# The second layer's gates, recurrence and merge in another order, queries before values, and split copies, in a four-layer fp32 kernel

## The chip, the cores and the metric

The kernel runs on one core of one Trainium2 chip, as one program. The metric is the device time of one execution in microseconds (us). The kernel before takes 789.82 us, the median of three runs (787.8 to 791.66).

## The reference

A tensor of 2 x 32 x 32 x 64 goes through four layers, each a residual of the last, all in fp32. What the change touches is in three of them:

```python
# second layer: 16 steps of a linear recurrence with constant gates, closed here
forget_gate = sigmoid(x @ Wf + bf + 2.0); input_gate = sigmoid(x @ Wi + bi)
delta = softplus(x @ Wd + bd) * 0.1
inp_r = delta_r * input_gate_r * Bx_r          # Bx = B * x, complex
step: h_r, h_i = fg_r * (Ar*h_r - Ai*h_i) + inp_r, fg_i * (Ar*h_i + Ai*h_r) + inp_i
# third layer: linear attention
q = softmax(q, -1) / sqrt(32); k = softmax(k, 0); out = (k^T v)^T q @ w_out
# fourth layer: four sweeps of attention without a softmax, over the Gram matrix of the tokens
Z = Z + sum_heads (Z Q Z^T)(Z V^T) / (n * heads)
```

## The kernel before, in words

Each engine runs its own list of instructions in the order in which the code of its block gives them, with waits on semaphores written out by hand (`sig(name)`); no scheduler moves anything. What stands late in an engine's list is late, ready or not. A wait is fulfilled when another engine has counted the semaphore up. The on-chip tiles of all stages lie in one array, `area`, and the eight PSUM banks are `ps`; the profile names them by these two words alone.

The first layer (a selective scan, 128 units) takes the first 463 us. The work around the change comes after it:

- **Gates.** VectorE (DVE) normalizes x into `xn1` (L1223). TensorE (PE) makes four products of four matmuls each (L1576 to L1581): `split` (x parted in real and imaginary halves) first, then the delta gate in banks 4 and 5, the forget gate in 0 and 1, the input gate in 2 and 3, and counts `gates_done` after each. ScalarE (ACT) takes Abs, Exp and Ln of the delta gate (L967 to L974), then loads another table of functions and takes the sigmoids of f and i (L975 to L981). The relu part of the softplus is DVE's (L364).
- **Recurrence** (L342 to L413, DVE). Each step is a 2 x 2 real matrix; its trace `tau` and determinant `det` come from the product and sum of the forget gates, and powers and sums of 2, 4, 8 and 16 steps follow by doubling. Squares are ACT's (L991 to L1002). Sums of `m` and `n` go through PE (`add_parts`). `tt` and `stt` issue an operation of two tensors; with `hold` DVE waits until it has ended.
- **Segments.** PE also mixes, between these, four segments of the fourth layer's filter weights (L1592 to L1598), each read out by ACT (`span_out`, L987) before the next one starts.
- **Merge.** `m` and `v` are put back into the layout of x by PE: four matmuls for `m` once all of DVE's closing work but the two products in `v` is done (`joined` 1), then two for each half of `v` (L1607 to L1616). DVE adds the result to x (L1234), PE turns it (L1623), and the third layer's norm begins (L432 to L444) while PE runs six matmuls that nobody reads (`keep_busy`, L1632).
- **Attention.** PE makes the keys' logits (L1638), then queries and values tile by tile in turn (L1645), in two halves. DVE shifts the queries (L1258, L1259), ACT takes Exp (L1025) and copies values (L1023) and turned keys (L1029), DVE makes the shares (L1267 to L1269), and PE turns them (L1668), multiplies by the mixed context (L1676) and turns the result (L1683).
- **Linear layers** (`for l in range(LAYERS)`, L1338, L1051, L1715): a chain of small products with a PSUM read-out behind each: `copy_g` (L479) makes two copies for `g_two` and one for `g_sb`, then PE makes t in bank 3, ACT copies all 512 columns of it (L1053), PE makes s (L1725).

## Time and profile before

| what | value |
|---|---|
| median of three runs | 789.82 us (787.8 to 791.66) |
| the profiled execution: its time, its span | 790.21 us, 788.4 us |
| mean granted clock of TensorE | 0.977 |
| PE busy | 90% of the span |
| VectorE busy | 77% |
| GpSimd, ScalarE busy | 52%, 44% |
| first layer | about 463 us |
| gates, recurrence, merge (463 to 511) | about 48 us |
| attention to its last turned tile (511 to 547) | about 36 us |
| linear layers (598 to 621) | about 23 us |

### The profile page before, as it was taken

The numbers are of one execution on the slowest core, as the hardware profiler recorded it, in microseconds if no ns is written. First come the engines' busy times: TensorE is split into PE (matmuls) and PEld (weight loads), VectorE is DVE, ScalarE is ACT, GpSimd is POOL, SyncE is SP. The second block draws the span as 40 slices with busy tenths as digits, with TensorE's granted clock in tenths as the row PEclk, the third lists the DMA queues.
The fourth block names the chain that finished last, engine by engine and source line by source line (L and its number), as shares of the span: only waits on it lengthen the run. The fifth ranks groups of instructions, "written<-read, shape, count | busy, mean of one in ns | idle before, by whom it ended". The sixth has DMA issues, their size and how long they took to land.

```text
span 788.4 us, 7109 instructions
## 1 busy us (share of the span) xinstructions
PE 713.4 (90%) x2480; PEld 358.9 (46%) x2480; DVE 605.7 (77%) x598; ACT 349.9 (44%) x387; POOL 413.4 (52%) x229
## 2 busy tenths in 40 slices
PE   6979999989899899998988868997798899999997
PEld 4633333333233233333333323465345577777775
DVE  5799999999999999999999948656793543334432
ACT  3676474556754754556544326143103243333331
POOL 3166999998999999899889900000051000000000
PEclk9979999999999999999999989999999999999999
DMA  5134564665554646536465451300730000000000
GB/s 169 62 133 140 185 212 168 220 214 175 187 180 166 236 162 207 197 137 202 157 246 176 159 214 81 106 10 1 281 145 1 1 0 1 1 1 0 0 0 27
DMA packets 30126, 97.76 MB, mean 124 GB/s; under 512 B 4132, under 2 KB 4870, under 8 KB 29358
## 3 DMA queue, kind: packets, MB, share of 16 engines
q1 hardware_dynamic: 30096, 97.38, 35.6%
q8 instruction: 16, 0.26, 0.1%
q14 instruction: 14, 0.11, 0.0%
HBM read 95.78 MB, written 1.59 MB: 123 GB/s over the span
## 4 chain that ended last, share of the span: by engine, by line
PE 42%; DVE 28%; issue 11%; POOL 9%; DMA 5%; ACT 4%; SPq 0%; DVEq 0%; POOLq 0%
PE ps L1765 15%; DVE area L1173 10%; PE ps L1460 6%; POOL area L617 6%; DVE ps L1161 5%; DMA area<-c_rows 4%; PE ps L1483 4%; PE ps L1781 4%; DVE area L1169 2%; DVE area L354 2%; PE ps L1386 2%; PE ps L1404 1%; DVE small L432 1%; POOL area L633 1%; PE ps L1451 1%
## 5 line engine op out<-in xcount | busy, mean ns | idle before, releaser
L617 POOL TENSOR_TENSOR area<-area 128x1024 f32<-128x1024 f32 x127 | 297.7, 2370 | 32.0 <-DVE area L1173 21.4
L1483 PE MATMUL ps<-area,cst 128*128 128x512 f32 x512 | 254.2, 623 | 7.1 <-POOL area L617 6.6
L1173 DVE TENSOR_TENSOR_SCAN area<-area,ps 128x1024 f32<-128x1024 f32 x111 | 249.8, 2275 | 4.1 <-ACT area L809 0.9
L809 ACT ACTIVATE area<-area,floors,par_sb 128x1024 f32<-128x1024 f32 x111 | 133.0, 1235 | 62.2 <-DVE area L1173 55.6
L1483 PEld LDWEIGHTS ps<-area,cst 128*128 128x128 f32 x512 | 89.8, 192 | 119.9 <-issue 95.5
L1161 DVE TENSOR_TENSOR ps<-ps,area 128x1024 f32<-128x1024 f32 x111 | 133.0, 1213 | 4.5 <-PE ps L1451 3.9
L1765 PE MATMUL ps<-stack,sel 128*128 128x512 f32 (+1 forms) x576 | 116.2, 362 | 0.7 <-DVE sel L1366 0.7
L1765 PEld LDWEIGHTS ps<-stack,sel 128*128 128x128 f32 x576 | 97.0, 191 | 19.7 <-issue 1.2
L464 DVE COPY area<-ps 64x1024 f32<-64x1024 f32 x32 | 39.3, 1227 | 73.6 <-PE ps L1781 41.4
L714 POOL COPY area<-area 128x256 f32 (+1 forms) x16 | 6.4, 403 | 131.3 <-PE ps L1781 131.3
L462 ACT ACTIVATE area<-ps 64x1024 f32<-64x1024 f32 x32 | 32.7, 1021 | 95.7 <-PE ps L1765 52.8
L1451 PE MATMUL ps<-stack,sel 32*128 32x512 f32 x222 | 54.1, 498 | 18.0 <-DVE area L1173 17.8
L695 POOL TENSOR_TENSOR area<-area 128x256 f32<-128x256 f32 x8 | 5.8, 728 | 120.5 <-DVE area L1319 120.5
L1451 PEld LDWEIGHTS ps<-stack,sel 32*128 32x128 f32 x222 | 20.3, 186 | 95.8 <-DVE area L1173 53.0
L1460 PE MATMUL ps<-area,cst 128*128 128x512 f32 x112 | 50.2, 600 | 6.3 <-DVE area L1173 6.3
L809 ACT ACTIVATE ps<-area,floors,par_sb 128x1024 f32<-128x1024 f32 x17 | 20.5, 1208 | 79.2 <-DVE area L1173 79.2
L1386 PE MATMUL ps<-cst 128*128 128x512 f32 (+1 forms) x110 | 45.0, 551 | 0.0
L633 POOL TENSOR_TENSOR area<-area 128x1024 f32<-128x1024 f32 x17 | 40.0, 2355 | 0.0
L1169 DVE TENSOR_TENSOR_SCAN area<-ps,area 128x1024 f32<-128x1024 f32 x17 | 38.5, 2267 | 0.0
L1460 PEld LDWEIGHTS ps<-area,cst 128*128 128x128 f32 x112 | 20.6, 190 | 34.8 <-issue 23.2
L1354 DVE TENSOR_TENSOR stack<-area,stack 128x1025 fp32r<-128x1025 f32 x16 | 19.5, 1227 | 14.8 <-ACT stack L1070 14.8
L1386 PEld LDWEIGHTS ps<-cst 128*128 128x128 f32 x110 | 21.9, 207 | 17.7 <-issue 16.5
(310 smaller groups left out, 713.2 us busy)
## 6 DMA issues: line engine op xcount, KB each, us to landing
area<-c_rows SPq DMA_DIRECT2D x145, 512.0 KB, 4.4
area<-phi_scaled SPq DMA_DIRECT2D x1, 4104.0 KB, 24.2
area<-in_m_phi_dram SPq DMA_DIRECT2D x4, 1024.0 KB, 8.2
area<-phi_scaled SPq DMA_DIRECT2D x1, 4096.0 KB, 13.8
area<-in_q_t_dram SPq DMA_DIRECT2D x1, 1024.0 KB, 13.7
c_rows<-tok SPq DMA_DIRECT2D x28, 32.0 KB, 2.8
area<-in_dft_dram SPq DMA_DIRECT2D x1, 784.0 KB
area<-in_m_u_dram SPq DMA_DIRECT2D x1, 768.0 KB, 5.8
```

The lines of the kernel that those rows point to most:

```text
L464: engine.tensor_copy(dst, src).then_inc(sig("filtered_1"), 1)
L617: pool.tensor_tensor(scan_order(prod[:, u % PRODS, :], k), lines(state[:, u % STATES, :], k), lines(c_sb[:, u % COPIES, :], k), MUL).then_ ...
L633: pool.tensor_tensor(aid, aid, u_in[:, n % 2, :], MUL).then_inc(sig("pool_driven"), 1)
L809: act.activation(dst, delta[:, n % 2, :], ACT.Exp, bias=floors[:, k, i:i + 1], scale=par_sb[:, k, i:i + 1]).then_inc(sig("decayed"), 1)
L1161: dve.tensor_tensor(drive_pair(u), drive_pair(u), u_in[:, n % 2, :], MUL).then_inc(sig("driven"), 1)
L1169: dve.tensor_tensor_scan(state[:, u % STATES, :], banks(BANK["a", u]), aid, 0.0, MUL, ADD).then_inc(sig("scanned"), 1)
L1173: dve.tensor_tensor_scan(state[:, u % STATES, :], decay[:, u % DECAYS, :], drive_pair(u), 0.0, MUL, ADD).then_inc(sig("scanned"), 1)
L1386: pe.matmul(ps[:, bank, 0:cols], ident, cst[:, 0:cols], start=True, stop=True)
L1451: mm = pe.matmul(ps[:, BANK["b", u] + h, :], sel[at:at + 32, i, :], b_rows[at:at + 32, n % 2, :], start=True, stop=True)
L1460: mm = pe.matmul(ps[:, BANK["soft", n] + h, :], ident, half(term, h), start=(at == 0), stop=(at == 3))
L1483: mm = pe.matmul(ps[:, 6 + h, :], con("center"), half(prod[:, u % PRODS, :], h), start=(u % (UNITS // 2) == 0), stop=(u % (UNITS // 2) == ...
L1765: mm = pe.matmul(ps[:, 2 + 2 * (g % 2) + y, :].rearrange("p (a n) -> p a n", a=2)[:, :, P * (at - 2 * y):2 * P], xn_hl[:, x_part, j * P:(j ...
```

## The change

Six things, all in the order of work or in who does it:

1. PE runs four matmuls that nobody reads before the product that averages the statistics of x (`pair_mean`) and two after it, and `keep_busy(5, ...)` before the merge has four in place of two.
2. The gates come in the order split, f, i, delta. ACT loads the sigmoids' table at once, takes both sigmoids, loads the other table, then takes Abs, the square of tau, Exp and Ln. DVE's products of f come before the relu, which is written straight into `v`. Since the logarithm now lives longer in `sp_a`, `sum4` and `p4` trade their tile with `r4_sq` and `lam4`, and ACT's square of `r4` waits until the logarithm has been read (`x_parts` 3).
3. `m * sum16` comes two operations earlier and alone counts `joined` 1. PE merges only the first half of `m`; DVE adds its second half to `v` before `joined` 3. Two matmuls fewer, one DVE addition of 512 columns more.
4. The last segment goes behind the merge, in place of five of the six idle matmuls, and its read-out behind ACT's part of the norm.
5. In attention, a half's queries are all made before its values, and the shares of the first half come before the shift of the second. ACT takes Exp of the first half's queries before it copies the values.
6. In the linear layers `g_ready` is counted before the copy into `g_sb`, and t is made in two banks, of which DVE copies one and ACT the other.

```diff
-        sum4, p4 = halves(sp_a)
+        sum4, p4 = halves(xn1)
...
-        r4_sq, lam4 = halves(xn1)
+        r4_sq, lam4 = halves(sp_a)
...
             dve.wait_ge(sig("gates_out"), 1)
-            for half_r in range(2):
-                link(dve.tensor_scalar(sp_r[...], ps[:, 4 + half_r, :], ..., 0.0, ADD, MAX), half_r == 1)
-            dve.sem_inc(sig("x_parts"), 1)
-            dve.wait_ge(sig("gates_out"), 2)
-            tt(v, r, lg, ADD)
-            dve.wait_ge(sig("gates_out"), 3)
             tt(p8_sq, f[:, 0, :], f[:, 1, :], ADD, False)
...
-            dve.wait_ge(sig("gates_out"), 4)
-            tt(v, v, i, MUL, False)
             tt(gap, tau, det, SUB, False)
+            dve.wait_ge(sig("gates_out"), 3)
+            for half_r in range(2):
+                link(dve.tensor_scalar(sp_v[...], ps[:, 4 + half_r, :], ..., 0.0, ADD, MAX), half_r == 1)
+            dve.sem_inc(sig("x_parts"), 1)
...
-            stt(sum8, step4, 1.0, sum4, ADD, MUL, False)
+            dve.wait_ge(sig("gates_out"), 4)
+            tt(v, v, lg, ADD, False)
+            stt(sum8, step4, 1.0, sum4, ADD, MUL)
+            dve.sem_inc(sig("x_parts"), 1)
+            tt(v, v, i, MUL)
...
-            tt(low16, det, sum16, MUL, False)
+            tt(low16, det, sum16, MUL)
+            dve.tensor_tensor(m, m, both(sum16), MUL).then_inc(sig("joined"), 1)
             tt(r16, r16, r8_sq, SUB)
-            tt(m, m, both(sum16), MUL, False)
             tt(low16, r16, low16, SUB)
-            dve.sem_inc(sig("joined"), 1)
-            for half_r in range(2):
-                dve.scalar_tensor_tensor(v[:, half_r, :], low16, 1.0, v[:, half_r, :], ADD, MUL).then_inc(sig("joined"), 1)
+            dve.scalar_tensor_tensor(v[:, 0, :], low16, 1.0, v[:, 0, :], ADD, MUL).then_inc(sig("joined"), 1)
+            stt(v[:, 1, :], low16, 1.0, v[:, 1, :], ADD, MUL)
+            dve.wait_ge(sig("joined"), 1)
+            dve.tensor_tensor(v[:, 1, :], v[:, 1, :], m[:, 1, :], ADD).then_inc(sig("joined"), 1)
...
-                copy(g_two[at, b, at], src[own, own], *extra)
-            copy(g_sb[own, own], src[own, own], *extra).then_inc(sig(f"g_ready_{b}"), 1)
+                ins = copy(g_two[at, b, at], src[own, own], *extra)
+            ins.then_inc(sig(f"g_ready_{b}"), 1)
+            copy(g_sb[own, own], src[own, own], *extra)
...
-                act.activation(t_sb, ps[:, 3, :], ACT.Copy).then_inc(sig("t_out"), 1)
+                act.activation(t_sb[:, 256:512], ps[:, 1, 0:256], ACT.Copy).then_inc(sig("t_out"), 1)
...
+                dve.wait_ge(sig("t_done"), l + 1)
+                dve.tensor_copy(t_sb[:, 0:256], ps[:, 3, 0:256]).then_inc(sig("t_out"), 1)
...
+            keep_busy(BANK["b", UNITS - 1], 4)
             pair_mean(2)
+            keep_busy(BANK["b", UNITS - 1], 2)
             pe.wait_ge(sig("gn_out"), 2)
...
+            def merged(src, r, last):
                 for h in range(2):
...
+                    mm = pe.matmul(ps[:, h, :], merge[:, h, r, :], src[:, r * HALF:(r + 1) * HALF],
+                                   start=not (r or last), stop=(r == 1))
...
+            pe.wait_ge(sig("joined"), 1)
+            merged(sp_m, 0, False)
+            pe.wait_ge(sig("joined"), 2)
+            merged(sp_v, 0, True)
+            pe.wait_ge(sig("joined"), 3)
+            merged(sp_v, 1, True)
...
-            keep_busy(4, 6)
+            segment(3)
+            keep_busy(4, 1)
```

**ACT, from the rstd of x to the first read-out of a segment.** `ps,small` is the forget gate, `ps,vecs` with a wait on `gates_done` the delta or the input gate. Before:

```order
L970 ACTIVATE area<-ps,vecs 128x512 [waits gates_done]
L970 ACTIVATE area<-ps,vecs 128x512
L973 ACTIVATE area<-area 128x1024 [waits gates_out]
L974 ACTIVATE area<-area 128x1024 [waits act_step]
L975 ACT_TABLE_LOAD
L980 ACTIVATE area<-ps,small 128x512 [waits gates_done]
L980 ACTIVATE area<-ps,small 128x512
L980 ACTIVATE area<-ps,vecs 128x512 [waits gates_done]
L980 ACTIVATE area<-ps,vecs 128x512
L982 ACT_TABLE_LOAD
L991 ACTIVATE area<-area 128x1024 [waits trace_set]
```

And now:

```order
L969 ACT_TABLE_LOAD
L974 ACTIVATE area<-ps,small 128x512 [waits gates_done]
L974 ACTIVATE area<-ps,small 128x512
L974 ACTIVATE area<-ps,vecs 128x512 [waits gates_done]
L974 ACTIVATE area<-ps,vecs 128x512
L976 ACT_TABLE_LOAD
L980 ACTIVATE area<-ps,vecs 128x512 [waits gates_done]
L980 ACTIVATE area<-ps,vecs 128x512
L983 ACTIVATE area<-area 128x1024 [waits trace_set]
L985 ACTIVATE area<-area 128x1024 [waits gates_out]
L986 ACTIVATE area<-area 128x1024 [waits act_step]
```

The two table loads stand before and behind the sigmoids as they did, but Abs, Exp and Ln have moved behind them, and the square of tau between Abs and Exp.

**DVE, from the product of bank 2 with f to the join with x.** Before:

```order
L354 TENSOR_TENSOR area<-ps,area 128x1024 [waits x_summed,dve_step]
L354 TENSOR_TENSOR area<-area 128x512 x2
L354 TENSOR_TENSOR area<-area 128x1024 [waits dve_step]
L354 TENSOR_TENSOR area<-area 128x512
L413 SCALAR_TENSOR_TENSOR area<-area 128x512 [waits dve_step]
L413 SCALAR_TENSOR_TENSOR area<-area 128x512
L1234 TENSOR_TENSOR area<-x_res,ps 128x2x128x2 [waits x_summed] x2
```

And now:

```order
L354 TENSOR_TENSOR area<-ps,area 128x1024 [waits x_summed,dve_step]
L354 TENSOR_TENSOR area<-area 128x512
L408 TENSOR_TENSOR area<-area 128x1024 [waits dve_step]
L354 TENSOR_TENSOR area<-area 128x512
L354 TENSOR_TENSOR area<-area 128x512 [waits dve_step]
L411 SCALAR_TENSOR_TENSOR area<-area 128x512 [waits dve_step]
L357 SCALAR_TENSOR_TENSOR area<-area 128x512
L414 TENSOR_TENSOR area<-area 128x512 [waits joined,dve_step]
L1242 TENSOR_TENSOR area<-x_res,ps 128x2x128x2 [waits x_summed] x2
```

The product of 1024 columns that PE waits for first is now the third operation and not the fourth, and an addition of 512 columns has come in before the join.

**DVE, the queries.** L1258 and L1266 are the maxima, L1267 (before) and L1272 (now) the sums of the shares. Before:

```order
L1258 TENSOR_REDUCE small<-ps 128x32 [waits qv_done]
L1259 TENSOR_TENSOR area<-ps,small 128x1024 [waits dve_step]
L1258 TENSOR_REDUCE small<-ps 128x32 [waits qv_done]
L1259 TENSOR_TENSOR area<-ps,small 128x1024 [waits dve_step]
L1262 TENSOR_SCALAR small<-small 128x1 [waits scalar_steps]
L1263 RECIPROCAL small<-small 128x1 [waits dve_step]
L1267 TENSOR_REDUCE small<-area 128x32 [waits q_exp,dve_step]
L1268 RECIPROCAL small<-small 128x32 [waits dve_step]
L1269 TENSOR_TENSOR area<-area,small 128x1024 [waits dve_step]
L1267 TENSOR_REDUCE small<-area 128x32 [waits q_exp]
```

And now:

```order
L1266 TENSOR_REDUCE small<-ps 128x32 [waits qv_done]
L1267 TENSOR_TENSOR area<-ps,small 128x1024 [waits dve_step]
L1272 TENSOR_REDUCE small<-area 128x32 [waits q_exp]
L1273 RECIPROCAL small<-small 128x32 [waits dve_step]
L1274 TENSOR_TENSOR area<-area,small 128x1024 [waits dve_step]
L1266 TENSOR_REDUCE small<-ps 128x32 [waits qv_done]
L1267 TENSOR_TENSOR area<-ps,small 128x1024 [waits dve_step]
L1280 TENSOR_SCALAR small<-small 128x1 [waits scalar_steps]
L1281 RECIPROCAL small<-small 128x1 [waits dve_step]
L1272 TENSOR_REDUCE small<-area 128x32 [waits q_exp,dve_step]
```

The first half's sum, reciprocal and product now stand ahead of the second half's maximum.

## Rows read from the trace of the kernel before

**Rows 1.** The page: busy time of the engines.

```profile
PE 713.4 (90%) x2480; PEld 358.9 (46%) x2480; DVE 605.7 (77%) x598; ACT 349.9 (44%) x387; POOL 413.4 (52%) x229
```

**Rows 2.** Windows: length; PE, PEld, DVE, ACT, POOL busy; granted clock; DMA share; GB/s.

```profile
465.90:472.10 6.20, 4.25 (x10) 1.24 (x12) 1.75 (x5) 0.50 (x2) 0.00 (x0) 0.51 1.00 424
541.00:544.40 3.40, 3.02 (x14) 2.08 (x14) 0.28 (x1) 1.02 (x1) 0.00 (x0) 0.52 0.00 0
485.00:490.00 5.00, 3.60 (x8) 1.33 (x8) 4.78 (x8) 2.61 (x5) 0.00 (x0) 1.00 0.00 0
```

**Rows 3.** Timeline of PE around the gates: start, us, engine, line, count, [idle before].

```profile
460.54 1.02 PE L1571 MATMUL ps<-area,w_out_w 128*64 128x512 f32 x2
...
465.35 0.38 PE L1381 MATMUL ps<-small,cst 128*128 128x2 f32 x2 [3.78 <-DVE small L1098]
467.85 3.68 PE L1579 MATMUL ps<-area,cst 128*64 128x512 f32 x8 [2.11 <-DVE area L1223]
```

**Rows 4.** Timeline of DVE from the copy of x to the join.

```profile
471.57 1.23 DVE L1225 COPY area<-ps 128x1024 f32<-128x1024 f32 x1 [3.78 <-PE ps L1579]
...
477.51 1.22 DVE L354 TENSOR_TENSOR area<-area 128x1024 f32<-128x1024 f32 x1 [0.66 <-ACT area L974]
480.16 2.62 DVE L354 TENSOR_TENSOR area<-area 128x512 f32<-128x512 f32 x4 [1.43 <-ACT area L980]
...
489.39 1.22 DVE L354 TENSOR_TENSOR area<-area,ps 128x1024 f32<-128x1024 f32 x1
...
499.30 1.23 DVE L354 TENSOR_TENSOR area<-ps,area 128x1024 f32<-128x1024 f32 x1
...
503.74 1.29 DVE L413 SCALAR_TENSOR_TENSOR area<-area 128x512 f32<-128x512 f32 x2
510.04 0.69 DVE L1234 TENSOR_TENSOR area<-x_res,ps 128x512 f32<-128x512 f32 x1 [5.01 <-PE ps L1614]
```

**Rows 5.** Timeline of ACT in the same stage.

```profile
477.49 1.28 ACT L975 ACT_TABLE_LOAD   x1
478.79 1.27 ACT L980 ACTIVATE area<-ps,small 128x512 f32<-128x512 f32 x2
```

**Rows 6.** Timeline of PE, recurrence and merge, and of DVE in the norm.

```profile
490.54 3.70 PE L1596 MATMUL ps<-area 128*128 128x512 f32 x8 [1.94 <-ACT area L987]
...
503.83 3.60 PE L1610 MATMUL ps<-area,cst 128*128 128x512 f32 x8
...
512.23 5.32 PE L1386 MATMUL ps<-cst 128*128 128x512 f32 x12
...
516.33 1.29 DVE L444 TENSOR_TENSOR area<-area,small 128x512 f32<-128x512 f32 x2
```

**Rows 7.** Timeline of ACT and PE, queries and values.

```profile
526.13 1.02 ACT L1023 ACTIVATE area<-ps 128x1024 f32<-128x1024 f32 x1
...
533.45 3.81 PE L1662 MATMUL ps<-area 128*128 128x128 f32 x32 [1.21 <-ACT area L1023]
```

**Rows 8.** Timeline of DVE, keys maximum, shares of the queries, next normalization.

```profile
523.99 0.15 DVE L1245 TENSOR_SCALAR small<-small 128x1 f32<-128x1 f32 x1
...
533.54 1.22 DVE L1259 TENSOR_TENSOR area<-ps,small 128x1024 f32<-128x1024 f32 x1
...
539.48 1.22 DVE L1269 TENSOR_TENSOR area<-area,small 128x1024 f32<-128x1024 f32 x1
...
547.23 0.89 DVE L432 BATCH_NORM_STATS2 small<-ps 128x6 f32<-128x64 f32 x6 [4.17 <-PE ps L1683]
```

**Rows 9.** Timeline of ACT and DVE in the third linear layer.

```profile
609.83 0.45 DVE L488 COPY area<-ps 64x64 f32<-64x64 f32 x2 [0.58 <-PE ps L1736]
...
611.73 0.60 ACT L1053 ACTIVATE area<-ps 128x512 f32<-128x512 f32 x1 [1.33 <-PE ps L1718]
...
614.61 0.29 DVE L1348 COPY area<-ps 128x128 f32<-128x128 f32 x1 [0.58 <-PE ps L1731]
```

**Rows 10.** DMA issues in 463.4:464.0, m_phi's last: KB, us to landing.

```profile
area<-in_m_phi_dram SPq DMA_DIRECT2D x1, 1024.0 KB, 11.2
```

More of the change, by code:

```diff
@@ L965, in pairs @@
                 return t.rearrange("p (r n) -> p r n", r=2)
-            act.wait_ge(sig("gates_done"), 2)
-            for r in range(2):
-                bias = vecs[:, V_BD + r:V_BD + r + 1]
-                ins = act.activation(pairs(sp_a)[:, r, :], ps[:, 4 + r, :], ACT.Abs, bias=bias)
-            ins.then_inc(sig("gates_out"), 1)
-            act.wait_ge(sig("gates_out"), 1)
-            link(act.activation(sp_a, sp_a, ACT.Exp, scale=-1.0))
-            act.activation(sp_a, sp_a, ACT.Ln, bias=1.0).then_inc(sig("gates_out"), 1)
             act.preload_act_table_set("sigmoid_and_others")
             for g, (dst, col) in enumerate(((sp_f, None), (sp_i, V_BI))):
-                act.wait_ge(sig("gates_done"), 3 + g)
+                act.wait_ge(sig("gates_done"), 2 + g)
                 for r in range(2):
@@ L982, in _ @@
             act.preload_act_table_set("natural_log_exp_and_others")
+            act.wait_ge(sig("gates_done"), 4)
+            for r in range(2):
+                bias = vecs[:, V_BD + r:V_BD + r + 1]
+                ins = act.activation(pairs(sp_a)[:, r, :], ps[:, 4 + r, :], ACT.Abs, bias=bias)
+            ins.then_inc(sig("gates_out"), 1)
+            act.wait_ge(sig("trace_set"), 1)
+            act.activation(sp_o, sp_d, ACT.Square).then_inc(sig("trace_sq"), 1)
+            act.wait_ge(sig("gates_out"), 3)
+            link(act.activation(sp_a, sp_a, ACT.Exp, scale=-1.0))
+            act.activation(sp_a, sp_a, ACT.Ln, bias=1.0).then_inc(sig("gates_out"), 1)
             def span_out(i):
@@ L988, in span_out @@
                                banks(6).rearrange("p (k e) -> p k e", k=KF), ACT.Copy).then_inc(sig("m_added"), 1)
-            act.wait_ge(sig("trace_set"), 1)
-            act.activation(sp_o, sp_d, ACT.Square).then_inc(sig("trace_sq"), 1)
             span_out(0)
@@ L996, in _ @@
             act.wait_ge(sig("trace_sq"), 1)
-            act.activation(r4_sq, r4, ACT.Square)
-            act.activation(det2, det, ACT.Square).then_inc(sig("fourth_sq"), 1)
+            act.activation(det2, det, ACT.Square)
+            act.wait_ge(sig("x_parts"), 3)
+            act.activation(r4_sq, r4, ACT.Square).then_inc(sig("fourth_sq"), 1)
             span_out(1)
@@ L1269, in _ @@
                 dve.tensor_tensor(q, q, rep, MUL).then_inc(sig("q_ready"), 1)
+            q_shift(0)
+            q_share(0)
+            q_shift(1)
+            dve.wait_ge(*after("k_exp"))
+            link(dve.tensor_scalar(small[:, 131:132], small[:, 130:131], float(B * L * np.sqrt(DH)), None, MUL))
+            link(dve.reciprocal(small[:, 131:132], small[:, 131:132]))
+            q_share(1)
             dve.wait_ge(*after("ctx_done"))
@@ L1572, in _ @@
                           start=True, stop=True).then_inc(sig("l0_half"), 1)
+            keep_busy(BANK["b", UNITS - 1], 4)
             pair_mean(2)
+            keep_busy(BANK["b", UNITS - 1], 2)
             pe.wait_ge(sig("gn_out"), 2)
-            for bank, lhs in ((6, split), (4, w_gate_sb[:, 2]), (0, w_gate_sb[:, 0]), (2, w_gate_sb[:, 1])):
+            for bank, lhs in ((6, split), (0, w_gate_sb[:, 0]), (2, w_gate_sb[:, 1]), (4, w_gate_sb[:, 2])):
                 for r in range(2):
@@ L1587, in add_parts, with segment @@
                 mm.then_inc(sig("x_summed"), 1)
-            pe.wait_ge(sig("m_in"), 64)
-            pe.wait_ge(sig("scaled_set"), 1)
-            pe.wait_ge(sig("x_out"), 1)
-            for i in range(4):
+            def segment(i):
                 wait(pe, sig("m_added"), i)
@@ L1598, in _ @@
                 mm.then_inc(sig("m_summed"), 1)
[L1599 to L1612 removed]
+            def merged(src, r, last):
                 for h in range(2):
[L1614 removed]
+                    mm = pe.matmul(ps[:, h, :], merge[:, h, r, :], src[:, r * HALF:(r + 1) * HALF],
+                                   start=not (r or last), stop=(r == 1))
                     if r == 1:
                         mm.then_inc(sig("x_summed"), 1)
+            pe.wait_ge(sig("m_in"), 64)
+            pe.wait_ge(sig("scaled_set"), 1)
+            pe.wait_ge(sig("x_out"), 1)
+            segment(0)
+            pe.wait_ge(sig("x_parts"), 2)
+            add_parts(4)
+            segment(1)
+            segment(2)
+            pe.wait_ge(sig("x_parts"), 4)
+            pe.wait_ge(sig("gates_out"), 2)
+            add_parts(2)
+            keep_busy(5, 4)
+            pe.wait_ge(sig("joined"), 1)
[4 more added lines that the diff above has]
+            merged(sp_v, 1, True)
             def turn(src, bank, made=0, what="normed"):
```

57 lines of the change are left out of this document (21 added, 36 removed).

## The prediction

> **What bounds the kernel now.** The page's first part shows PE at 90% and VectorE at 77% [rows 1]; PE's share includes idle matmuls and says nothing of the stages that the change touches. So I read the stages: the chain of waits from 463 to 621 us for whose turn it is, the timelines of PE, DVE and ACT for what each was idle for, and windows for the granted clock. The reader is to see a chain that hops between engines. In the gates PE is late, at the lower clock. In the recurrence DVE is the bound: idle twice for ACT and hardly ever after that. In the merge PE is the bound, with DVE idle for 5.01 us. In the attention and the linear layers nobody is full, and each read-out and each semaphore lies on the chain. 
>
> **Part 1, idle matmuls around the statistics.** PE stands idle for 3.78 us, makes one tiny product, and is idle for 2.11 us more; from 465.90 to 472.10 the granted clock is 0.51, 1.2 GHz [rows 2, 3]. The four matmuls of `split` begin at 467.85 and take 3.68 us; at twice the clock their stream is half as long, 1.72 us plus 0.17. DVE's copy of their result, at 471.57 [rows 4], would start at 469.75: **1.8 us**. The fillers themselves: four matmuls from 461.4 take 3.44 us and end at 464.9, before `pair_mean` can start at 465.35; the two behind it end at 467.4, before 467.85. Cover is thin, 0.45 us on each side, but at the upper clock they cost nothing. That they hold it: from 485 to 490 PE is busy 3.60 of 5.00 us and keeps 1.00 [rows 2], and it waits 1.94 us before 490.54 [rows 6] without a fall; now its longest idle here is about 0.5 us. Bounds: 0 and 1.8; I take 1.8. The segments' data land at 474.1 (issued 462.92, 11.2 us) [rows 10]; `segment` 0 now wants them at 474.75 instead of 477.3. That is a margin of 0.6 us, and behind it 3 us more before DVE needs `add_parts(4)`.
>
> **Part 2, sigmoids first.** DVE was idle 0.66 us for Ln and 1.43 us for the sigmoids of f [rows 4]. Now f's product ends at 471.4, its sigmoids (1.27 us) at 472.8, i's at 474.5, the table is there at 475.75, Abs at 477.0. DVE: copy at 469.75, `m` and `n` until 473.5, the four products of f (2.62) until 476.2, `gap` until 476.85, then 0.15 us of wait for Abs. Relu (1.41) runs until 478.5, and the square of tau, 477.0 to 478.05, is ready before that. Exp and Ln end at 480.2, and DVE asks for them at 482.5. The operations on DVE are the same in number. From the copy to the product with bank 4 it was 471.57 to 489.39, 17.8 us; now 15.85: **1.95 us**. The second segment's read-out waits for the square of `r4`, at 485.1; then `segment` 2 ends at 490.2, `add_parts(2)` at 493.7, and DVE asks at 495.55. The wait that comes in is hidden by 1.8 us. Bounds 1.6 and 2.1.
>
> **Part 3, the merge.** From the product with bank 2 at 499.30 to the join at 510.04 it was 10.74 us [rows 4]. PE had to pass four matmuls of `m` (from 503.83) and three of `v` [rows 6]. Now, counted from the same point: 1.14 + 0.73 + 1.22 us to `joined` 1 at +3.1; two matmuls until +4.9; `r16`, `low16` and the first product in `v` to `joined` 2 at +5.2; second product and addition (0.65 + 0.7; two such took 1.29 at 503.74) to `joined` 3 at +6.6; PE is busy with the first half of `v` until +6.95, and one matmul more gives `x_summed` at +8.0. **2.7 us**, bounds 2.3 and 3.0. PE's four idle matmuls end 1.6 us before `joined` 1.
>
> **Part 4, the last segment behind the merge.** Six idle matmuls from 512.23 took until 517.38, while the norm's first half was there at about 517.0 (half of 1.29 us behind 516.33) [rows 6]. Four of the segment and one filler end 0.86 us earlier, so the norm decides: **0.3 us**. The read-out on ACT, 1.0 us, fits between Exp of the norm and the turned tiles. Bounds 0 and 0.4.
>
> **Part 5, queries before values.** Before: maximum of the keys until 524.14, shift of the second half until 534.76, then both shares, 5.94 us, until 540.70 [rows 8]. Now on DVE from 524.2: queries are there (four groups of matmuls and not eight), shift 2.5 us, 526.7; Exp 1.06 (ACT is free at 526.13 [rows 7]), 527.8; share 2.9, 530.7; second shift, 533.2; Exp, 534.2; second share, 537.15. That is 3.55 us earlier. Who is late next? ACT, whose first copy of values moves from 526.13 to 527.7 and makes the last one end at 532.7, so that PE's 3.81 us of context [rows 7] end at 536.7, 0.5 us before the share. Then the tail: before, 540.70 to 547.23 = 6.5 us, in which the clock was 0.52 from 541.00 to 544.40 with PE busy 3.02 us [rows 2]. PE came there after two waits for shares; now it comes from the context with hardly a gap, so I take 1.0: the tail is 5.2 us. **4.85 us**, bounds 2.0 (values late by the length of a copy, clock low) and 4.9.
>
> **Part 6, linear layers.** `g_ready` comes one copy earlier, half of 0.45 us; t's read-out, 0.60 us for 512 columns on ACT, becomes 256 columns on two engines, between 0.29 (128 columns) and 0.60, I take 0.42 from the first two [rows 9]. 0.22 + 0.18 = 0.4 us in each of four layers: **1.6 us**, bounds 0.8 and 1.9.
>
> **Sum.** 1.8 + 1.95 + 2.7 + 0.3 + 4.85 + 1.6 = 13.2 us. The profiled execution took 790.21 us, 0.4 over the median of 789.82, so 777.0 from the one and 776.6 from the other; I say 777.0.
>
> **Two rules weighed.** After the table load at 477.49 (1.28 us) the sigmoid starts at 478.79, 0.02 us later [rows 5]. The Trainium skill, "ScalarE: Activation LUTs", What ACT_TABLE_LOAD costs, gives 1.28 us for the load and a drain of about 1.38 us besides; by it the sum would be about 11.8. The trace agrees on the load and shows no such drain.
>
> The stretch at 1.2 GHz from 541.00 follows one in which PE did little but turn the queries' tiles, with waits for the shares between [rows 2, 8]. The Trainium skill, "TensorE: Matmul & The Clock Gate", Part 4 on transposes, says that transposing doesn't count as busy for the clock. The row cannot tell that from mere idleness.
>
> **The rivals.**
> - *The clock falls before the gates all the same* (12%): the fillers leave gaps of half a microsecond, and where the clock was held, gaps were up to 1.94 us, which speaks against it. Part 1 gives 0: 778.8.
> - *The clock falls in the attention's tail all the same* (10%): turned tiles still stand right before it, 16 of them with two small gaps. 1.3 us back: 778.3. This is the way in which the page on the clock gate would have it.
> - *Table load with a drain behind it* (4%): the second switch now stands on the path, before Abs, and DVE has only 0.15 us of slack there. If ACT stood still for as long as the load takes again, 1.3 us: 778.3. Against it: the 0.02 us above. It is the page on activation tables that would have it.
> - *Values late* (6%): ACT takes one Exp before the first copy, PE's second half of values waits for it, and context and turning end after the share. Part 5 gives some 2.5 us less: 779.5.
> - *Slower* (2%): one mechanism, the clock in the recurrence. PE now has less slack than DVE's chain there: 16 gate matmuls, three segments, two sums, fillers, merge. If the clock fell at the gates and the waits behind (0.4, 1.2 and 1.6 us) kept it at 0.50, the gates would end at 481.6, and five groups of four at 6.9 us each put the second sum at 516, the join at about 531 instead of 510: 21 us lost against 6.5 won behind it, 805. It decides from the point where the second sum ends later than DVE asks, a loss of 1.8 us on PE. Against it: 485 to 490 at 1.00.
>
> The forecast itself, with small errors in its terms, has 62%; 4% are for sums between 8 and 10 us for no reason listed.
>
> **How the numbers follow.** Range: the low end takes every upper bound (14.2 us off 789.8) and the 1.9 us by which runs lie off their median, 774.0. The high end takes both clock rivals and the lower bound of part 6 (about 9.3 us) and 1.5 us of spread, 782.0. A measurement of this kernel can tell about 0.5%, 3.9 us, from no change. Every case but the last gives over 8 us: faster 0.95, same 0.03, slower 0.02.
>
> **What would show it.** In the windows, granted clock 1.00 from 462 to 475 and in the tail of the attention. On DVE: copy of x at 469.8, no idle over 0.3 us until the product with bank 2 at 495.6, the join at 503.6 after about 2 us of idle. First row of the attention's norm at about 535.6. Layers about 0.4 us shorter each. Wrong if the join comes after 506, if DVE waits for `add_parts(2)`, if PE waits after the context for a share by more than 1 us, or if t's two copies take as long as one did.

## The result, and the profile after

The changed kernel takes 776.99 us, the median of four runs (776.64 to 778.22), against 790.32 us for the kernel before (787.8 to 791.66): a ratio of 0.9838, with a 95% interval of 0.981 to 0.9865. The profiled execution took 776.8 us, its span is 775.0 us where it was 788.4. The page after:

```profile
span 775.0 us, 7121 instructions
...
PE 710.9 (92%) x2482; PEld 357.2 (46%) x2482; DVE 607.2 (78%) x603; ACT 349.0 (45%) x387; POOL 413.5 (53%) x229
```

Windows of the profile after; the columns are length, PE, PEld, DVE, ACT and POOL busy, granted clock, DMA share, GB/s:

```profile
core 0: us, PE busy (x) PEld busy (x) DVE busy (x) ACT busy (x) POOL busy (x), PEclk, DMA share, GB/s
462.00:475.00 13.00, 12.56 (x47) 4.37 (x46) 9.37 (x15) 5.17 (x8) 0.00 (x0) 1.00 1.00 402
530.00:536.00 6.00, 5.42 (x37) 3.42 (x36) 1.18 (x5) 3.31 (x4) 0.00 (x0) 1.00 0.01 3
...
551.30:558.10 6.80, 6.80 (x16) 3.89 (x16) 4.23 (x15) 0.31 (x1) 0.00 (x0) 0.53 1.04 397
620.00:626.00 6.00, 5.26 (x27) 4.24 (x25) 2.10 (x3) 2.46 (x5) 0.00 (x0) 1.00 0.00 0
```

The first two answer to [rows 2]: the gates and the attention's tail now run at 1.00. In the third the clock is down over the router's products, where it was up in the profile before. The last is the beginning of the last stage, where the kernel before was at the lower clock for a time:

```profile
633.20:636.60 3.40, 3.40 (x11) 2.72 (x10) 0.00 (x0) 0.04 (x1) 0.00 (x0) 0.51 0.00 0
```

PE in the same places as in [rows 3, 6]:

```profile
461.10 3.70 PE L1401 MATMUL ps<-cst 128*128 128x512 f32 x8
464.95 0.38 PE L1396 MATMUL ps<-small,cst 128*128 128x2 f32 x2
465.19 1.96 PE L1401 MATMUL ps<-cst 128*128 128x512 f32 x4
467.44 1.94 PE L1596 MATMUL ps<-area,cst 128*64 128x512 f32 x8 [0.29 <-DVE area L1231]
469.21 5.32 PE L1596 MATMUL ps<-area,w_gate_sb 128*64 128x512 f32 x24
...
486.51 3.70 PE L1611 MATMUL ps<-area 128*128 128x512 f32 x8 [1.11 <-ACT area L991]
...
493.48 3.60 PE L1401 MATMUL ps<-cst 128*128 128x512 f32 x8
498.68 5.75 PE L1617 MATMUL ps<-area,cst 128*128 128x512 f32 x12 [1.61 <-DVE area L408]
...
529.87 1.91 PE L1692 MATMUL ps<-cst,area 128*128 128x128 f32 x16
...
532.33 1.94 PE L1700 MATMUL ps<-area 128*64 128x512 f32 x8 [0.38 <-DVE area L1287]
```

The four idle matmuls end at 464.8, the two behind the statistics at 467.15, and `split` takes 1.94 us where it took 3.68. PE waits 1.11 us for ACT's read-out and 1.61 us for `m`. Six matmuls are left of the merge's eight (x12). The queries' sixteen tiles are turned in one go.

DVE, the rows that answer to [rows 4, 8]:

```profile
466.57 0.81 DVE L1231 TENSOR_SCALAR area<-x_res,small 128x1024 f32<-128x1024 f32 x1 [0.60 <-ACT small L964]
469.43 1.23 DVE L1233 COPY area<-ps 128x1024 f32<-128x1024 f32 x1 [2.04 <-PE ps L1596]
470.78 5.12 DVE L354 TENSOR_TENSOR area<-area 128x1024 f32<-128x1024 f32 x6
...
476.74 1.41 DVE L372 TENSOR_SCALAR area<-ps,vecs 128x512 f32<-128x512 f32 x2
...
483.55 0.68 DVE L357 SCALAR_TENSOR_TENSOR area<-area 128x512 f32<-128x512 f32 x1
484.37 1.22 DVE L354 TENSOR_TENSOR area<-area 128x1024 f32<-128x1024 f32 x1
485.63 1.22 DVE L354 TENSOR_TENSOR area<-area,ps 128x1024 f32<-128x1024 f32 x1
...
495.54 1.22 DVE L354 TENSOR_TENSOR area<-ps,area 128x1024 f32<-128x1024 f32 x1
...
497.40 1.22 DVE L408 TENSOR_TENSOR area<-area 128x1024 f32<-128x1024 f32 x1
...
501.31 0.69 DVE L414 TENSOR_TENSOR area<-area 128x512 f32<-128x512 f32 x1
503.62 0.69 DVE L1242 TENSOR_TENSOR area<-x_res,ps 128x512 f32<-128x512 f32 x1 [1.61 <-PE ps L1617]
...
517.30 0.15 DVE L1253 TENSOR_SCALAR small<-small 128x1 f32<-128x1 f32 x1
...
525.16 1.22 DVE L1267 TENSOR_TENSOR area<-ps,small 128x1024 f32<-128x1024 f32 x1
...
529.21 1.22 DVE L1274 TENSOR_TENSOR area<-area,small 128x1024 f32<-128x1024 f32 x1
...
535.75 2.20 DVE L433 BATCH_NORM_STATS2 small<-ps 128x6 f32<-128x64 f32 x16 [3.47 <-PE ps L1707]
```

From the copy of x on DVE is idle for 0.16 us at a time at most, until it waits for the join, 1.61 us instead of 5.01. ACT, to [rows 5], and its Exp of the second half's queries:

```profile
474.14 1.28 ACT L976 ACT_TABLE_LOAD   x1
475.44 1.27 ACT L980 ACTIVATE area<-ps,vecs 128x512 f32<-128x512 f32 x2
...
526.41 1.06 ACT L1031 ACTIVATE area<-area 128x1024 f32<-128x1024 f32 x1 [0.33 <-DVE area L1267]
```

And the linear layers, DVE first, then ACT, to [rows 9]:

```profile
598.75 0.45 DVE L489 COPY area<-ps 64x64 f32<-64x64 f32 x2 [0.58 <-PE ps L1760]
...
600.42 0.42 DVE L1353 COPY area<-ps 128x256 f32<-128x256 f32 x1 [0.97 <-PE ps L1742]
```

```profile
587.43 0.45 ACT L489 ACTIVATE area<-ps 64x64 f32<-64x64 f32 x2
587.79 0.21 ACT L491 ACTIVATE area<-ps 64x64 f32<-64x64 f32 x1
...
600.42 0.38 ACT L1061 ACTIVATE area<-ps 128x256 f32<-128x256 f32 x1 [1.11 <-PE ps L1742]
```

Two engines copy t at the same moment, in 0.42 and 0.38 us.

**Where the time went**, from starts of rows in each profile. The columns: start of x's normalization (the end of the first layer); from there to the copy of x; to the product with bank 4; to the product with bank 2; to the join; to the keys' maximum (the last small operation on it); to the next norm's first statistics; to the first copy of the Gram matrix; to the add of the linear layers' result; to the end of the span.

| profile | x norm | copy | bank 4 | bank 2 | join | keys | norm | Gram | add | end |
|---|---|---|---|---|---|---|---|---|---|---|
| before | 466.98 | 4.59 | 17.82 | 9.91 | 10.74 | 13.95 | 23.24 | 49.24 | 28.15 | 163.78 |
| after | 466.57 | 2.86 | 16.20 | 9.91 | 8.08 | 13.68 | 18.45 | 50.21 | 26.78 | 162.26 |
| `b_fill` | 467.79 | 2.85 | 17.07 | 9.90 | 10.75 | 13.94 | 21.83 | 49.25 | 28.13 | 162.29 |
| `a_nofill` | 467.28 | 4.60 | 16.73 | 9.91 | 8.07 | 13.69 | 18.45 | 49.48 | 26.77 | 163.62 |
| `a_gates_old` | 466.95 | 2.86 | 17.07 | 9.91 | 8.07 | 13.68 | 18.46 | 49.23 | 26.77 | 162.30 |
| `a_merge_old` | 467.57 | 2.85 | 16.22 | 9.91 | 10.70 | 13.70 | 18.45 | 49.24 | 26.79 | 162.27 |
| `a_attn_old` | 468.55 | 2.85 | 16.21 | 9.91 | 8.08 | 13.69 | 21.83 | 49.24 | 26.77 | 163.77 |
| `b_attn_fill` | 467.57 | 4.60 | 17.44 | 9.91 | 10.74 | 13.95 | 21.83 | 49.95 | 28.14 | 162.27 |
| `a_t_old` | 466.78 | 2.85 | 16.21 | 9.92 | 8.07 | 13.69 | 18.46 | 49.23 | 27.46 | 162.23 |
| `a_lin_old` | 466.70 | 2.86 | 16.21 | 9.91 | 8.07 | 13.69 | 18.45 | 49.26 | 28.14 | 162.31 |
| `a_fill8` | 469.60 | 2.85 | 16.22 | 9.91 | 8.07 | 13.69 | 18.44 | 50.00 | 26.79 | 162.23 |
| `a_no_merge_fill` | 466.87 | 2.85 | 16.21 | 9.91 | 10.61 | 13.69 | 18.46 | 49.24 | 26.78 | 162.28 |
| `a_more` | 467.56 | 2.85 | 16.21 | 9.90 | 8.07 | 13.70 | 18.45 | 49.38 | 26.78 | 162.30 |
| `a_turn_fill` | 466.93 | 2.85 | 16.21 | 9.91 | 8.07 | 13.69 | 18.46 | 50.19 | 26.78 | 162.31 |

Where nothing was changed and the clock was the same, a stage agrees to 0.02 us in most profiles; so a stage's length says more than a median: the runs of one changed version spread over 1.4 to 7.3 us, those of the kernel before over up to 10.1. Where the clock fell inside a stage, that no longer holds: the stage to bank 4 took 17.82 us before and 17.44 in `b_attn_fill`, with the same instructions. The granted clock was back at 1.00 at 472.9 and 472.7, which is 5.9 and 5.2 us after x's normalization began. The first layer, which no version changes, ends between 466.57 and 468.55 (`a_fill8` aside). Before less after, by column: 0.41 + 1.73 + 1.62 + 0 + 2.66 + 0.27 + 4.79 - 0.97 + 1.37 + 1.52 = 13.40 us.

### The profile page after: what moved, and what is told of

Its sections match the earlier page's. It is cut to its first block, busy times and chain, and to the rows that moved or that the text cites. A ratio compares the mean times of both kernels' runs of the same rounds, so it can differ in the third digit from the quotient of the medians.

```text
span 775.0 us, 7121 instructions
## 1 busy us (share of the span) xinstructions
PE 710.9 (92%) x2482; PEld 357.2 (46%) x2482; DVE 607.2 (78%) x603; ACT 349.0 (45%) x387; POOL 413.5 (53%) x229
## 4 chain that ended last, share of the span: by engine, by line
PE 43%; DVE 28%; issue 12%; POOL 10%; DMA 3%; ACT 3%; DVEq 0%; SPq 0%; POOLq 0%
PE ps L1789 15%; DVE area L1181 9%; PE ps L1498 7%; POOL area L619 6%; PE ps L1475 6%; DVE ps L1169 4%; PE ps L1805 4%; DVE area L354 3%; DMA area<-c_rows 2%; DVE area L1177 2%; PE ps L1466 2%; DVE small L433 1%; PE ps L1419 1%; POOL area L635 1%; DVE area L1332 1%
## 5 line engine op out<-in xcount | busy, mean ns | idle before, releaser
L1401 PE MATMUL ps<-cst 128*128 128x512 f32 (+1 forms) x116 | 47.8, 552 | 0.0
```

The costliest lines, as they stand in the source:

```text
L1401: pe.matmul(ps[:, bank, 0:cols], ident, cst[:, 0:cols], start=True, stop=True)
```

## The experiments

Each effect is read in the column of the table where it belongs. No experiment undoes part 4 by itself; between the join and the keys' maximum it is the only thing that the change touches.

**`b_fill`**: the six idle matmuls of part 1 alone, on the kernel before (without the two more ahead of the merge).

```diff
+            keep_busy(BANK["b", UNITS - 1], 4)
             pair_mean(2)
+            keep_busy(BANK["b", UNITS - 1], 2)
```

Expected: 

> The kernel before with part 1 alone: four idle matmuls ahead of the statistics' product and two behind it. Theory: they hold the clock at 1.00 from 462 to 475, DVE's copy of x starts 2.9 us after the normalization of x began instead of 4.6, and the time falls by 1.8 us, to about 788.5 against 790.3. But the delta gate leads in this kernel and ACT's logarithm and sigmoids follow it, so part of the 1.8 us holds only if ACT is moved forward as well: since all of ACT's work hangs on the same four products, it should be. Rival A: the stretch at the lower clock only moves to a later place where it costs as much, and the time stays at 790.3. Rival B: the fillers end too late and the statistics wait for them, +0.4 us or more.

Measured: 786.86 us against 789.97, ratio 0.9956 (0.9934 to 0.9977). The copy comes 1.74 us sooner, and the next stage is 0.75 us shorter too, at 17.07 (0.37 shorter than in `b_attn_fill`): idle matmuls alone are worth 2.1 to 2.5 us in the old order, by where the lower clock lies. That the fillers hold the clock here is well borne out: all three profiled kernels without them (before, `a_nofill`, `b_attn_fill`) have it fall at 465.9 to 466.0, and none of the eleven with them has it fall between the last units of the first layer and the merge. In this profile the clock is also up in the attention's tail and in the last stage, so part of the median's 3.1 us need not be theirs. Rivals A and B fall.

**`a_nofill`**: the changed kernel without the six.

```diff
-            keep_busy(BANK["b", UNITS - 1], 4)
             pair_mean(2)
-            keep_busy(BANK["b", UNITS - 1], 2)
```

Expected: 

> The changed kernel without the six idle matmuls around the statistics. Theory: the clock falls to 0.50 between 466 and 472, copy of x starts 1.7 us later, and as the gates are longer by 2 to 3 us, ACT's second table load, Abs and with them DVE's relu are later still: the time rises by 1.7 to 3.5 us, to 778.7 to 780.5. Rival: the gates run at the upper clock without the fillers too (another place of the stretch in this run), and the time stays at 777.0.

Measured: 779.33 us (0.9855 of before, 0.982 to 0.989). The clock is at 0.51 from 465.9 to 472.8. DVE's rows show the theory's second half as well:

```profile
471.88 1.23 DVE L1233 COPY area<-ps 128x1024 f32<-128x1024 f32 x1 [3.78 <-PE ps L1594]
...
479.71 1.41 DVE L372 TENSOR_SCALAR area<-ps,vecs 128x512 f32<-128x512 f32 x2 [0.51 <-ACT area L980]
```

The copy waits as before, and Abs is late by 0.51 us. 1.74 + 0.53 = 2.27 us. The medians differ by 2.34, an agreement closer than runs that spread over 2 us can bear out.

**`a_gates_old`**: part 2 undone.

```diff
-            for bank, lhs in ((6, split), (0, w_gate_sb[:, 0]), (2, w_gate_sb[:, 1]), (4, w_gate_sb[:, 2])):
+            for bank, lhs in ((6, split), (4, w_gate_sb[:, 2]), (0, w_gate_sb[:, 0]), (2, w_gate_sb[:, 1])):
```

with the old order on ACT and on DVE up to the sum of eight. Expected: 

> The changed kernel with part 2 undone (delta gate first, its logarithm before the sigmoids, the old order on DVE up to the sum of eight). Theory: DVE is idle twice again, for the logarithm and for the sigmoids of f, and the stretch from the copy of x to the product with bank 4 is 1.6 us longer (16.2 to 17.8): 778.6. With the clock up, PE is no longer late for ACT, but ACT's own chain (Abs, Exp, Ln, table load, sigmoids) is 5.0 us long whatever the clock, so the idle stays. Rival: the two idles were PE's doing at the lower clock, and with the fillers in place the old order costs nothing: 777.0.

Measured: 777.57 us (0.9844 of before, 0.9805 to 0.9882). Both were wrong: the stage is 17.07 us long, 0.87 more than 16.20 and 0.75 less than 17.82.

```profile
469.81 1.23 DVE L1232 COPY area<-ps 128x1024 f32<-128x1024 f32 x1 [2.04 <-PE ps L1595]
...
475.23 1.23 DVE L354 TENSOR_TENSOR area<-area 128x1024 f32<-128x1024 f32 x1 [0.15 <-DVE area L365]
477.66 2.62 DVE L354 TENSOR_TENSOR area<-area 128x512 f32<-128x512 f32 x4 [1.20 <-ACT area L982]
```

Of the two idles the one for the logarithm (0.66) was PE's doing at the lower clock; the one for the sigmoids of f stayed at 1.20 of 1.43. At the upper clock the order itself is worth 0.87 us.

**`a_merge_old`**: part 3 undone, with the old order on DVE and of the merge's matmuls; the last segment stays where the change puts it.

```diff
-            dve.tensor_tensor(m, m, both(sum16), MUL).then_inc(sig("joined"), 1)
...
-            dve.tensor_tensor(v[:, 1, :], v[:, 1, :], m[:, 1, :], ADD).then_inc(sig("joined"), 1)
...
-            merged(sp_m, 0, False)
...
+            for h in range(2):
+                for r in range(2):
+                    pe.matmul(ps[:, h, :], merge[:, h, r, :], sp_m[:, r * HALF:(r + 1) * HALF], start=(r == 0), stop=False)
...
```

Expected: 

> The changed kernel with part 3 undone (all of m merged by PE, after all of DVE's closing work), the last segment still behind the merge. Theory: the stretch from the product with bank 2 to the join is 10.7 us instead of 8.1 and the time rises by 2.6 us to 779.6. Rival: part of what the new merge gained came from the last segment being out of its way (before, it and two idle matmuls ended just as m was ready), so that with the segment gone the old merge costs under 2 us.

Measured: 780.53 us (0.9888 of before, 0.9848 to 0.9928), the stage 10.70 us, 2.62 more than 8.08 and within 0.04 of the 10.74 before. The theory holds, and the rival falls: the last segment was not in the old merge's way. The median is 3.5 us up, 0.9 more than the stage accounts for, with runs from 779.51 to 785.65.

**`a_attn_old`**: part 5 undone, on DVE, ACT and PE. On ACT:

```diff
-            query(0)
-            value(0)
+            v_and_q(0)
...
-            value(1)
-            query(1)
+            v_and_q(1)
```

Expected: 

> The changed kernel with part 5 undone (queries and values tile by tile, both shifts before both shares). Theory: from the keys' maximum to the last share's end it is 16.7 us again instead of 13.1, so 3.4 to 3.6 us are lost whatever the clock does; the 1.2 to 1.4 us of the tail (from the last share to the next norm's first statistics, 6.5 us before, 5.3 after) come back only if the clock falls there. So 780.5 with the tail at the upper clock, 781.8 with it at the lower. Rival: most of the 4.8 us was the tail's clock and what is left of the reordering is under 2.5 us.

Measured: 783.08 us (0.9914 of before, 0.9872 to 0.9956). The stage is 21.83 us, with the clock up: the order of queries, values and shares is worth 3.38 us. The median is 6.1 us above the changed kernel's; of that this profile has 1.5 in the last stage, where the clock fell (0.50 from 625.9 to 629.3), and 2.0 in the first layer, before any changed instruction, with two falls there that the changed kernel's profile lacks (at 216 and 373). Of the five runs the one with a mean granted clock of 0.990 took 778.67 us, the four at 0.977 to 0.979 took 782.74 to 785.93.

**`b_attn_fill`**: two idle matmuls in the kernel before.

```diff
             for h in range(2):
+                if h == 1:
+                    keep_busy(6, 2)
                 pe.wait_ge(sig("q_ready"), h + 1)
```

Expected: 

> The kernel before with two idle matmuls (1.7 us) between the turning of the first and the second half of the queries, where PE waits 1.68 us for the second share, and nothing else. Theory: PE's idleness there is what lets the clock fall at 541; with the fillers the tail runs at 1.00 and takes 5.1 to 5.3 us instead of 6.5, the time falls by 1.3 us at most (some runs of the kernel before have no fall there anyway). Rival, by the Trainium skill, TensorE: Matmul & The Clock Gate, Part 4, where transposes do not count as busy: the turning itself keeps the engine idle in the chip's eyes, and the tail stays at 0.50.

Measured: 788.51 us against 789.76, ratio 0.9987 (0.997 to 1.0004). PE:

```profile
538.20 1.09 PE L1670 MATMUL ps<-cst,area 128*128 128x128 f32 x8 [0.72 <-DVE area L1269]
539.13 1.88 PE L1386 MATMUL ps<-cst 128*128 128x512 f32 x4
540.98 1.10 PE L1670 MATMUL ps<-cst,area 128*128 128x128 f32 x8
541.91 0.33 PE L1673 MATMUL ps<-area 128*128 128x64 f32 x2
542.62 1.94 PE L1678 MATMUL ps<-area 128*64 128x512 f32 x8 [0.38 <-DVE area L1274]
```

The products with the context take 1.94 us for x8 where [rows 2] had them at the lower clock, and the stage is 21.83 us instead of 23.24: the clock was worth 1.41 us. But `b_fill`, which changes nothing here, has 21.83 too. So one profile each doesn't show that these fillers hold it, and theory and rival both stay open here. The interval of the ratio takes in 1.

**`a_t_old`, `a_lin_old`**: t in one bank, copied by ACT (the first piece); and in the second the early `g_ready` undone as well.

```diff
-                act.activation(t_sb[:, 256:512], ps[:, 1, 0:256], ACT.Copy).then_inc(sig("t_out"), 1)
+                act.activation(t_sb, ps[:, 3, :], ACT.Copy).then_inc(sig("t_out"), 1)
...
-                dve.wait_ge(sig("t_done"), l + 1)
-                dve.tensor_copy(t_sb[:, 0:256], ps[:, 3, 0:256]).then_inc(sig("t_out"), 1)
...
-                ins = copy(g_two[at, b, at], src[own, own], *extra)
-            ins.then_inc(sig(f"g_ready_{b}"), 1)
-            copy(g_sb[own, own], src[own, own], *extra)
+                copy(g_two[at, b, at], src[own, own], *extra)
+            copy(g_sb[own, own], src[own, own], *extra).then_inc(sig(f"g_ready_{b}"), 1)
```

Expected of the first: 

> The changed kernel with t in one bank and copied by ACT alone, g_ready still early. Theory: t's copy is 0.60 us instead of 0.42, so 0.18 us in each of four layers, 0.7 us together: 777.7, and 27.5 us from the first copy of the Gram matrix to the add of the layers' result instead of 26.8. Rival: two engines reading PSUM at once slow each other, and the split was worth nothing: 777.0.

Expected of the second: 

> The changed kernel with part 6 undone. Theory: 28.15 us from the first copy of the Gram matrix to the add, as before, instead of 26.8; of the 1.37 us, 0.7 are t's split copy and 0.65 the early g_ready: 0.22 in each of the two layers in which DVE releases PE, 0.11 in the two in which ACT does, since ACT's third copy overlaps the second by half. 778.4. Rival: the parts are not additive, because with t late the filler behind it covers g_sb's copy.

Measured: 777.18 and 777.75 us (0.9837 and 0.9843 of before), the stage 27.46 and 28.14 us against 26.78. That is 0.68 us for t's copy and 0.68 for `g_ready`, and they add up. The medians alone, 0.2 and 0.8 us above the changed kernel's, would not have told.

**`a_fill8`**: eight idle matmuls ahead of the statistics.

```diff
-            keep_busy(BANK["b", UNITS - 1], 4)
+            keep_busy(BANK["b", UNITS - 1], 8)
             pair_mean(2)
```

Expected: 

> The changed kernel with eight in place of four idle matmuls ahead of the statistics' product. Theory: the cover is 3.85 us long (461.1 to 464.95) and four fill 3.5 of it, so four more push the product back by 3.1 us and everything behind it: 780.1, and 5.9 to 6.0 us from the start of DVE's statistics to the normalization of x instead of 3.3 (it was 3.34 before). Rival: DVE's own work is the longer chain and hides part of it: under 2 us.

Measured: 780.79 us (0.9877 of before, 0.984 to 0.9913).

```profile
461.11 7.13 PE L1401 MATMUL ps<-cst 128*128 128x512 f32 x16
468.08 0.28 PE L1396 MATMUL ps<-small,cst 128*128 128x2 f32 x2
```

The fillers begin at 461.11, as in the changed kernel, and take 7.13 us; the statistics' product, at 464.95 with four of them, starts at 468.08: 3.1 us late, and x's normalization 3.03 us. The rival falls, and the cover's length is confirmed.

**`a_no_merge_fill`**: no idle matmuls before the merge.

```diff
-            keep_busy(5, 4)
```

Expected: 

> The changed kernel without the four idle matmuls before the merge, so that PE is idle from 493.5 to 498.7, 5.2 us, instead of 1.6. Theory: the clock falls to 0.50 over the merge, its six matmuls take up to twice 0.86 us each, and the join comes 2 to 4 us later (8.1 us from the product with bank 2 become 10 to 12), with the turning and the last segment slower too: 779 to 781. Rival: the clock does not follow a single gap of this size and the time stays at 777.0.

Measured: 779.51 us (0.986 of before, 0.9825 to 0.9894), the stage 10.61 us instead of 8.08.

```profile
498.97 8.30 PE L1617 MATMUL ps<-area,cst 128*128 128x512 f32 x12 [5.04 <-DVE area L408]
```

Six matmuls take 8.30 us instead of 5.75, and the window over them is at the lower clock:

```profile
498.00:504.80 6.80, 5.83 (x7) 2.52 (x8) 4.19 (x6) 0.00 (x0) 0.00 (x0) 0.50 0.19 58
```

Four matmuls that nobody reads are worth 2.53 us against none. The kernel before had two here and no fall; whether the two that part 1 adds were needed was not tried.

**`a_turn_fill`**: the fourteen idle matmuls ahead of the router's turning as transposes.

```diff
-            keep_busy(0, 14)
+            for _ in range(112):
+                pe.transpose(ps[:, 0, 0:P], ident, ident)
```

Expected: 

> The changed kernel with its longest row of idle matmuls (fourteen, 12 us, ahead of the turning for the router) replaced by 112 transposes of the identity into the same bank, equally long at the upper clock. Theory A (transposes count as work for the clock): the granted clock stays at 1.00 over them and each takes 0.11 us, nothing moves. Theory B (the Trainium skill, TensorE: Matmul & The Clock Gate, Part 4: they do not): the clock falls to 0.50 within them, they take more than 12 us, so that the turning for the norm is late by up to 9 us, and the time rises by 3 to 10 us.

Measured: 777.19 us in a single run. PE's row, then two windows:

```profile
535.92 12.39 PE L1711 MATMUL ps<-cst 128*128 128x128 f32 x112
```

```profile
538.00:542.00 4.00, 4.00 (x39) 4.00 (x38) 3.83 (x12) 0.53 (x2) 0.00 (x0) 1.00 0.00 0
542.00:546.00 4.00, 4.00 (x39) 4.00 (x38) 3.82 (x16) 0.00 (x0) 0.00 (x0) 1.00 0.15 53
```

112 transposes in 12.39 us, 0.11 us each, at a granted clock of 1.00. Theory A: in this execution fp32 transposes keep the clock up. The Trainium skill, "TensorE: Matmul & The Clock Gate", Part 4, says of transposes, on figures for bf16, that they don't count as busy in the same way; here the measurement decides. So the stretch at 0.52 from 541.0 in the kernel before can't be laid to the turning as such. What made the clock fall there is not shown.

**`a_more`**: more cover where the clock still falls.

```diff
-            keep_busy(0, 14)
+            keep_busy(0, 15)
...
-            keep_busy(6, 7)
+            keep_busy(6, 8)
             turn(tile(xn), 0, 10)
+            keep_busy(6, 1, 256)
```

Expected: 

> The changed kernel with a fifteenth idle matmul before the router's norm is turned, an eighth before the last stage, and a half one (256 columns) between the last turning and the first convolution. The clock fell in the changed kernel's profile at 551.3 over the router's small products (2.90 us instead of 1.96, 0.97 us lost) and in the kernel before at 633.2 over the first convolutions (1.5 us lost), each after a stretch in which PE had turned tiles and waited. Theory: in both places the fillers leave 0.2 us of idleness where there was 1.05 and 1.5, the falls there become rarer, and the median falls by 0.3 to 1.0 us, to 776.0 to 776.7; where no fall would have been, nothing changes (50.2 to 49.2 us from the attention's norm to the first copy of the Gram matrix). Rival: transposes do not count as busy and one filler more does not decide, so the falls stay as frequent: 777.0. Rival: the fillers end too late and delay the turning, +0.2 to 0.6 us.

Measured: 777.63 us (0.9841 of before, 0.9813 to 0.9869): no gain. In its profile the router ran at the upper clock, but the clock was down from 559 on, over the experts' products. The stage was 49.38 us, 0.14 over the 49.24 of `a_no_merge_fill`; DVE runs nearly without idle there. Whether the fillers did that or the execution would have gone so anyway, one profile doesn't tell. No version had a lower median than the changed kernel.

## Why the prediction was right

It said 777.0 us and a range of 774.0 to 782.0; 776.99 was measured. The mechanisms came as forecast, but that the total is right to 0.01 us is luck: its parts fell short by 0.8 us, and places that the change does not touch made up for it.

- **Part 1**, 1.8 us forecast: 1.73. The fillers' ends (464.9 and 467.4 forecast) were 464.8 and 467.15, the copy 469.43 with a first layer 0.41 us shorter.
- **Part 2**, 1.95 forecast: 1.62. The step that failed is "the operations on DVE are the same in number": so they are, but DVE now waits for the end of two more of them (`sum8` and `v * i`). Where nothing is waited for, the next operation starts before the one ahead ends, as in the kernel before, where the product with bank 4 starts at 489.39 [rows 4], 0.08 us before the end of this one:

```profile
488.78 0.69 DVE L357 SCALAR_TENSOR_TENSOR area<-area 128x512 f32<-128x512 f32 x1
```

In the rows after, 484.37 starts 0.14 us behind the end of 483.55 (a semaphore is counted up between them as well), and 485.63 starts 0.04 behind the end of 484.37. That is 0.22 and 0.12 us, and explains the 0.33 in full. And the credit was wrong: I gave all of it to the order. `a_gates_old` puts 0.87 us to the order at the upper clock (1.20 us of idle less these 0.34), and what is left, 0.75 in this pair of profiles, to the clock. That does not alter the sum, since both were made.
- **Part 3**, 2.7 forecast: 2.66, and 2.62 by `a_merge_old`. `joined` 1 at +3.1 was right to 0.05 us (PE starts at 498.68, 3.14 behind 495.54), and DVE waits 1.61 us.
- **Part 4**, 0.3 forecast: 0.27.
- **Part 5**, 4.85 forecast: 4.79. The second share was to end 13.16 us after the keys' maximum (537.15 less 523.99); it ended 13.13 us after (530.43 less 517.30). The tail was 5.32 us for the 5.2 forecast. Only 3.38 us of this is the order's, for 3.55 forecast; 1.41 is a fall of the clock that the kernel before has in its profile, and that `b_fill` and `b_attn_fill`, with the same order, don't have. I had treated it as a fixed cost of the kernel before. That this fall was in the profile from which the forecast was made, and not in the one after, is luck as well.
- **Part 6**, 1.6 forecast: 1.37. The term that was mis-sized is `g_ready`, put at 0.22 in all four layers; by `a_lin_old` it gave 0.68 in all. In the first two ACT is the one that releases PE, and on ACT the third copy overlaps the second: 587.43 + 0.45 for two, 587.79 + 0.21 for the third, so that it ends only 0.12 us behind them. t's copy was 0.17 us a layer, 0.18 forecast.
- **What the sum did not hold**: -0.97 us at the router and +1.52 us in the last stage, both the clock's, and 0.41 us in the first layer. They come to 0.96 us, a little more than the 0.8 us by which the parts fell short.

One slip in the prediction's working changed little: the upper bounds add up to 14.1 us and not 14.2, and the low end that they give is 773.8.

Of the rivals, the two on the clock, the drain behind the table load and the late values can be seen not to have come in this profile. The load at 474.14 takes 1.28 us and Abs starts at 475.44, so a drain shows no more than it did in [rows 5]. (The Trainium skill, "ScalarE: Activation LUTs", What ACT_TABLE_LOAD costs, gives one of about the load's own length; no run here shows it.) The slower rival needed the clock to fall at the gates and stay low in the recurrence. `a_nofill` shows the first without the second: 0.51 from 465.9 to 472.8, and 1.00 from 472.9 to 500, over an idle of 1.11 us. In `a_no_merge_fill` one idle of 5.04 us made the clock fall over the merge, and it was up again for the last segment.

What stays open: what makes the clock fall in the attention's tail, at the router and in the last stage, and how often it does. Only profiled executions show the places, but each run has its mean granted clock on record. Of 42 runs of the kernel before, the four at 0.982 and above took 786.44 to 788.0 us, and the 31 at 0.977 and below took 788.68 to 796.5. So part of the spread between runs goes with the clock.

## What to carry to other kernels

In a chain that hops between engines, write out every instruction's start by hand from the rows' durations: the stages here came within 0.13 us of it, apart from two waits of DVE for itself (0.33 us) and copies that overlap on ACT (0.2). Compare variants by the length of stages between the same rows of their profiles, which repeated to 0.02 us where the clock was up, and not by medians that spread over several. Fill TensorE's waits with work that nobody reads where products on the path follow, but measure the cover first: four in a cover of 3.85 us, with two behind them, gave 2.3 us, and eight took 3.0.
